# SiLU of the FFN's output moved to the FFN's end, and the gate product of the last heads moved to GpSimd

## What is computed

```python
x = L0_attn_x
xn = _layernorm(x, axis=-1)
s = _L0_attn_ref(xn, Wq, Wk, Wv, Wo, q_norm_w, k_norm_w)   # ends in out @ Wo.T
g = _silu(_L0_ffn_ref(xn, gate_w, ..., down_s))            # (silu(x@gate) * (x@up)) @ down
return x + s * g
```

## Time and profile before

| what | value |
|---|---|
| median of 3 runs | 1312.06 us (1311.99 to 1312.15) |
| the profiled execution | 1312.74 us, of which the span is 1310.9 us |
| TensorE busy | 1282.3 us, 98% of the span |
| VectorE, ScalarE, GpSimd busy | 74%, 50%, 53% |
| granted TensorE clock, mean | 0.997 |
| head, in the steady part | about 30 us |

### The profile page before, as it was taken

How to read it: one execution, slowest core, us unless ns; L and a number is a source line. 1 busy time by engine, 2 the same in 40 slices (tenths; PEclk the granted TensorE clock), 3 DMA queues, 4 the chain that set the end, 5 groups by cost and what they waited for, 6 DMA issues and landing times.

```text
span 1310.9 us, 21024 instructions
## 1 busy us (share of the span) xinstructions
PE 1282.3 (98%) x7135; PEld 1100.7 (84%) x7135; DVE 975.9 (74%) x2087; ACT 653.0 (50%) x1427; POOL 699.3 (53%) x747
## 2 busy tenths in 40 slices
PE   8999999999999999999999999999999999999996
PEld 7788888887888888888888888888888888888875
DVE  7455555577888777877787778777877787778887
ACT  4322222245565555555555555555555555555552
POOL 4755555544555455545554555455545554546444
PEclk9999999999999999999999999999999999999998
DMA  6554554020010000000000000000000000000031
GB/s 186 155 142 122 135 130 132 19 81 17 17 34 17 17 17 33 18 17 18 33 17 19 21 28 18 22 21 25 22 19 26 22 19 21 20 10 24 9 129 65
DMA packets 30909, 62.08 MB, mean 47 GB/s; under 512 B 3808, under 2 KB 3808, under 8 KB 30560
## 3 DMA queue, kind: packets, MB, share of 16 engines
q1 hardware_dynamic: 30816, 60.88, 16.1%
HBM read 56.67 MB, written 4.19 MB: 46 GB/s over the span
## 4 chain that ended last, share of the span: by engine, by line
PE 89%; DVE 6%; issue 2%; DMA 1%; POOL 1%; ACT 1%; SPq 0%; DVEq 0%; ACTq 0%; POOLq 0%
PE O L1025 31%; PE O L1086 15%; PE S L1572 11%; PE T L1046 10%; PE S L1068 5%; PE S L1066 5%; PE S L1065 5%; DVE pb L794 2%; PE T L1105 2%; PE O L1588 1%; PE T L1588 1%; PE O L1586 1%; PE T L1586 1%; PE O L1587 1%; PE T L1587 1%
## 5 line engine op out<-in xcount | busy, mean ns | idle before, releaser
L415 POOL TENSOR_TENSOR pb<-rel,coef 128x1024 f32<-128x1024 f32 (+7 forms) x256 | 293.8, 1162 | 133.0 <-PE T L1046 127.7
L536 ACT ACTIVATE pb<-pb,low 128x1024 f32<-128x1024 f32 (+7 forms) x256 | 198.9, 777 | 190.6 <-DVE low L794 188.5
L526 ACT ACTIVATE pt_h<-T 128x512 fp32r<-128x512 f32 (+3 forms) x384 | 186.0, 487 | 116.2 <-PE T L1046 113.1
L778 DVE TENSOR_TENSOR pt_l<-T,pt_h 128x512 fp32r<-128x512 f32 (+3 forms) x384 | 210.3, 550 | 40.7 <-ACT pt_h L526 40.5
L794 DVE CUSTOM_DVE_ANT_0 pb<-S,pb,ninv 128x1024 f32<-128x1024 f32 (+7 forms) x256 | 207.7, 811 | 37.8 <-PE S L1068 32.2
L1046 PE MATMUL T<-ident,pb 128*128 128x128 f32 x1152 | 189.2, 274 | 12.7 <-DVE pb L803 5.7
L1046 PEld LDWEIGHTS T<-ident,pb 128*128 128x128 f32 x1152 | 140.7, 140 | 50.8 <-issue 13.5
L803 DVE TENSOR_SCALAR pb<-pb,rinv 128x1024 f32<-128x1024 f32 (+7 forms) x256 | 171.0, 668 | 9.0
L1065 PE MATMUL S<-kT_h,q_h 128*128 128x512 f32 (+2 forms) x384 | 141.4, 368 | 0.0
L1086 PE MATMUL O<-pt_h,v_h 128*128 128x512 f32 (+2 forms) x384 | 140.6, 366 | 0.0
L375 POOL TENSOR_TENSOR wo_l<-wo_in,wo_h 128x512 fp32r<-128x512 f32 x32 | 41.6, 1298 | 181.0 <-ACT wo_h L573 181.0
(11 more groups left out here) (163 smaller groups left out, 2884.9 us busy)
## 6 DMA issues: line engine op xcount, KB each, us to landing
wq_in<-in_wq SPq DMA_DIRECT2D x32, 256.0 KB, 2.8
wo_in<-in_wo SPq DMA_DIRECT2D x32, 256.0 KB, 2.6
stage<-in_wkv SPq DMA_DIRECT2D x8, 512.0 KB, 3.9
pb<-in_gate_w SPq DMA_DIRECT2D x14, 256.0 KB, 2.6
pb<-in_gate_z SPq DMA_DIRECT2D x14, 256.0 KB, 3.6
pb<-in_gate_s SPq DMA_DIRECT2D x14, 256.0 KB, 5.0
pb<-in_up_w SPq DMA_DIRECT2D x14, 256.0 KB, 5.4
pb<-in_up_z SPq DMA_DIRECT2D x14, 256.0 KB, 6.1
```

The source lines that it names most:

```text
L415: g_.tensor_tensor(pbuf(idx, t), rel[:, TOK - w:TOK], coef[:, t:t + 1].to_broadcast([P, w]), ALU.mult).then_inc(bias_ready, 1)
L526: a_.activation(pt_lot(pt_h, t, n), bank[:, 0:m * P].rearrange("p (k w) -> p k w", w=P), ACT.Copy).then_inc(tr_hi, 1)
L536: a_.activation(pbuf(idx, t), pbuf(idx, t), ACT.Exp, bias=low[:, idx:idx + 1], scale=-1.0, accum_out=rsum[:, idx:idx + 1]).then_inc(exps_r ...
L778: v_.tensor_tensor(pt_lot(pt_l, t, n), bank[:, 0:m * P].rearrange("p (k w) -> p k w", w=P), f(pt_lot(pt_h, t, n)), ALU.subtract).then_inc( ...
```

## The change

1. SiLU is applied in place to each unit of `yT` at the FFN's end by ScalarE, right after VectorE's last sum of the unit; what goes to `y_dram` is SiLU(y). ScalarE's high part of the second group's k/v weights is made before it. There is no SiLU in the epilogue.
2. In even heads the output projections make the four units of token half 0, in odd heads those of half 1, so that the units of half 0 have their sum of heads 0 to 29 in head 30.
3. GpSimd makes x + sum x SiLU (`base`) for all eight units: unit 0 in head 30 after its last bias, units 2 and 4 in head 31 after its fourth bias, the other five after head 31's last bias. VectorE then does L994's and L997's work for all units (`finish`), and in the epilogue waits for GpSimd's base before the first of the two.
4. The loads of `x` and `y_dram` are split and partly issued in head 29. `x` goes in two halves to other places.
5. At the FFN's end TensorE's order is y units 0 to 3, scores(0, 0), y units 4 to 7, scores(0, 1), kv0, kv1, and then the transposes of tile 7. VectorE's order follows it.

```diff
+    BASES = [0, 2, 4, 1, 3, 5, 7, 6]
...
@@ SyncE @@
                 if last and j == PER - 1:
                     sp.wait_ge(out_ready, Places("last", g).n(f"qc0_{j}"))
-                    sp.wait_ge(y_out, 16 * KT * NC)
-                    sp.dma_start(keep["stage"][:, :], y_dram[:, 0:6 * CH]).then_inc(y_in, 16)
-                    sp.dma_start(xt[:, :, :], xT).then_inc(xt_in, 16)
+                    sp.dma_start(x_late[1][:, :, :], xT[:, :, CH:TOK]).then_inc(x_late_in[1], 16)
                     sp.wait_ge(tr_ready, part_no(h, "ss0") + 1)
-                    sp.dma_start(sq[:, :], y_dram[:, 6 * CH:8 * CH]).then_inc(y_in, 16)
+                    sp.dma_start(sq[:, :], y_dram[:, 6 * CH:8 * CH]).then_inc(y_in_sq, 16)
...
+                if last and j == 1:
+                    sp.wait_ge(y_out, 16 * KT * NC)
+                    sp.wait_ge(v_ready, GROUPS)
+                    sp.wait_ge(out_ready, Places("last", g).n("v1_0"))
+                    sp.dma_start(x_late[0][:, :, :], xT[:, :, 0:CH]).then_inc(x_late_in[0], 16)
+                    sp.dma_start(keep["stage"][:, :], y_dram[:, 0:6 * CH]).then_inc(y_in, 16)
...
@@ GpSimd @@
+        def base(u):
+            m, c = divmod(u, NC)
+            n = BASES.index(u)
+            pool.wait_ge(out_free, Places("last", GROUPS - 1).n(f"w{m}_{2 + c}"))
+            g_.tensor_tensor(part(sT, u), part(sT, u), y_part(u), ALU.mult).then_inc(base_ready, 1)
+            pool.wait_ge(base_ready, 2 * n + 1)
+            g_.tensor_tensor(part(sT, u), part(sT, u), x_part(u), ALU.add).then_inc(base_ready, 1)
...
                 bias(h, 2)
                 bias(h, 3)
+                if not more:
+                    base(BASES[1])
+                    base(BASES[2])
...
+                if last and j == 2:
+                    pool.wait_ge(x_late_in[0], 16)
+                    pool.wait_ge(y_in, 16)
+                    base(BASES[0])
...
         group(GROUPS - 1, "last")
-        pool.wait_ge(out_free, Places("last", GROUPS - 1).n(f"w3_{PER - 1}"))
-        pool.wait_ge(xt_in, 16)
-        for n, u in enumerate(FIN[4:]):
-            pool.wait_ge(silu_ready, 4 + n + 1)
-            g_.tensor_tensor(part(sT, u), part(sT, u), y_part(u), ALU.mult).then_inc(base_ready, 1)
-            pool.wait_ge(base_ready, 2 * n + 1)
-            g_.tensor_tensor(part(sT, u), part(sT, u), part(xt, u), ALU.add).then_inc(base_ready, 1)
+        pool.wait_ge(x_late_in[1], 16)
+        pool.wait_ge(y_in_sq, 16)
+        for u in BASES[3:]:
+            base(u)
...
@@ ScalarE @@
         steps()
+        wkv_hi_part(1)
+        silu()
...
         lots(HEADS - 1, 1)
         lots(HEADS - 1, 0)
-        silu(FIN[:4])
         v_hi(epi_at, "v0_0", PER - 1)
-        silu(FIN[4:])
...
+        def silu():
+            for u, (m, c) in enumerate(UNIT):
+                y = yT[:, m, c * CH:(c + 1) * CH]
+                act.wait_ge(y_added, (IT - 1) * UNITS + u + 1)
+                a_.activation(y, y, ACT.Silu).then_inc(silu_ready, 1)
...
@@ VectorE @@
         steps()
+        add(IT - 1, range(0, 4))
         logits(0, 0)
-        add(IT - 1, range(0, 4))
+        add(IT - 1, range(4, 8))
+        logits(0, 1)
         normalise(0, 0)
-        logits(0, 1)
-        add(IT - 1, range(4, 8))
...
-                    project(at, f"w0_{j}", unit, kind == "first")
+                    project(at, f"w0_{j}", 0 + j % 2, kind == "first")
...
+        def finish(u):
+            n = BASES.index(u)
             dve.wait_ge(out_ready, epi_at.n(f"w{u}"))
+            dve.wait_ge(base_ready, 2 * n + 1)
             v_.tensor_tensor(y_part(u), O[epi_at.bank(f"w{u}")][:, :], y_part(u), ALU.mult).then_inc(out_free, 1)
+            dve.wait_ge(base_ready, 2 * n + 2)
             dve.wait_ge(out_free, epi_at.n(f"w{u}"))
             v_.tensor_tensor(part(sT, u), part(sT, u), y_part(u), ALU.add).then_inc(fin, 1)
 
         normalise(HEADS - 1, 7)
-        project(epi_at, "w1", 1)
+        finish(1)
         lots(HEADS - 1, 1)
-        project(epi_at, "w3", 3)
+        finish(3)
         lots(HEADS - 1, 0)
-        project(epi_at, "w5", 5)
-        out_add(1)
+        finish(5)
         v_lo(epi_at, "v0_0", PER - 1)
-        out_add(3)
-        project(epi_at, "w7", 7)
-        out_add(5)
-        out_add(7)
-        for u in FIN[4:]:
-            out_last(u)
+        for u in FIN[3:]:
+            finish(u)
...
@@ TensorE @@
+        y_units(IT - 1, 1, range(0, 4))
         pe.wait_ge(sg_ready, IT * NC)
         scores(0, 0)
-        y_units(IT - 1, 1, range(0, 4))
+        y_units(IT - 1, 1, range(4, 8))
         pe.wait_ge(hid_ready, IT * NC)
         scores(0, 1)
-        y_units(IT - 1, 1, range(4, 8))
...
             if kind == "first":
-                pe.wait_ge(y_added, IT * KT * NC - 2)
+                pe.wait_ge(y_added, IT * KT * NC - 1)
+                kv_proj(at, "kv0", 1)
+                pe.wait_ge(y_added, IT * KT * NC)
+                kv_proj(at, "kv1", 1)
...
-                    project(at, f"w{n}_{j}", 4 * (j % 2) + n, h - 2 - j % 2, 0 if j >= 2 else 2,
+                    project(at, f"w{n}_{j}", 2 * n + j % 2, h - 2 - j % 2, 0 if j >= 2 else 2,
                             at.n(f"v0_{j - j % 2}"))
```

More of the change, by code:

```diff
@@ L266, in attention @@
     zeroed = sem("zeroed")
[L267 to L269 removed]
+    y_in, y_in_sq, x_late_in, base_ready, fin, stored = (
+        sem("y_in"), sem("y_in_sq"), [sem("x0_in"), sem("x1_in")], sem("base_ready"), sem("fin"), sem("stored"))
+    x_late = keep["x_late"]
     epi_at = Places("epi")
     FIN = [int(n[1]) for n in EPI if n[0] == "w"]
+    BASES = [0, 2, 4, 1, 3, 5, 7, 6]
     def part(tile, unit):
@@ L275, in part, with x_part @@
         return tile[:, m, c * CH:(c + 1) * CH]
+    def x_part(unit):
+        return x_late[unit % NC][:, unit // NC, :]
     def y_part(unit):
-        tile, n = (keep["stage"], unit) if unit < 6 else (sq, unit - 6)
+        slot = unit % NC * KT + unit // NC
+        tile, n = (keep["stage"], slot) if slot < 6 else (sq, slot - 6)
         return tile[:, n * CH:(n + 1) * CH]
@@ L620, in _ @@
         last_kv_squares()
-        weights, steps = feed.act(act)
+        weights, steps, silu = feed.act(act)
         act.wait_ge(qk_ready, 1)
@@ L649, in group @@
                     exp(h, 0)
-                elif kind != "last":
+                elif kind == "steady":
                     wkv_hi_part(g + 1)
@@ L900, in group @@
                 w = not (kind == "first" and j < 2)
-                unit = 4 * (j % 2)
                 if prev and j > 0:
@@ L937, in group @@
                 if w:
-                    project(at, f"w1_{j}", unit + 1, kind == "first")
+                    project(at, f"w1_{j}", 2 + j % 2, kind == "first")
                 if not prev:
@@ L949, in group @@
                 else:
-                    project(at, f"w2_{j}", unit + 2, kind == "first")
+                    project(at, f"w2_{j}", 4 + j % 2, kind == "first")
                 lot(h, 4, 0)
@@ L971, in group @@
                 if w:
-                    project(at, f"w3_{j}", unit + 3, kind == "first")
+                    project(at, f"w3_{j}", 6 + j % 2, kind == "first")
                 logits(h, 7)
@@ L977, in _ @@
         group(GROUPS - 1, "last")
[L978 to L985, removed]
-            v_.tensor_tensor(part(sT, u), part(sT, u), part(xt, u), ALU.add).then_inc(fin, 1)
-        def out_last(u):
-            n = FIN.index(u)
-            dve.wait_ge(silu_ready, n + 1)
-            dve.wait_ge(base_ready, 2 * (n - 4) + 1)
+        def finish(u):
+            n = BASES.index(u)
             dve.wait_ge(out_ready, epi_at.n(f"w{u}"))
+            dve.wait_ge(base_ready, 2 * n + 1)
             v_.tensor_tensor(y_part(u), O[epi_at.bank(f"w{u}")][:, :], y_part(u), ALU.mult).then_inc(out_free, 1)
-            dve.wait_ge(base_ready, 2 * (n - 4) + 2)
+            dve.wait_ge(base_ready, 2 * n + 2)
             dve.wait_ge(out_free, epi_at.n(f"w{u}"))
@@ L1264, in group @@
                 scores(h, 2)
-                if not prev:
-                    pe.wait_ge(y_added, IT * KT * NC)
-                    kv_proj(at, "kv0", 1)
                 w_unit(0)
                 lot(h, 6, 0)
-                if not prev:
-                    kv_proj(at, "kv1", 1)
                 w_unit(1)
@@ L1616, in program @@
         with ExitStack() as late:
-            late.enter_context(nc.sbuf_tensor("xt_pad", [P, KT, TOK], F32))
-            xt = late.enter_context(nc.sbuf_tensor("xt", [P, KT, TOK], F32))
+            late.enter_context(nc.sbuf_tensor("over_xh", [P, 224 + KT * TOK], F32))
+            over_xl = late.enter_context(nc.sbuf_tensor("over_xl", [P, KT, CH], F32))
+            late.enter_context(nc.sbuf_tensor("over_rest", [P, KT * CH + KT * TOK + 6 * CH], F32))
+            over_w0 = late.enter_context(nc.sbuf_tensor("over_w0", [P, KT, CH], F32))
         keep = {
-            "xt": xt,
+            "x_late": [over_w0, over_xl],
```

7 lines of the change are left out of this document (4 added, 3 removed).

## The result

The changed kernel takes 1310.28 us (median of 20 runs, 1309.46 to 1312.56), the kernel before beside it 1312.24 us (20 runs, 1311.7 to 1313.64): ratio 0.9984, 95% interval 0.9978 to 0.9991. So it is faster, by 1.96 us or 0.16%, where the prediction gave 4.6 us. That is just under the 0.2% that it had set as the bound of "faster". The profiled execution took 1310.9 us with a span of 1309.1; in the one of before the span is 1.8 us longer.

The account below looks back on a forecast made before the run. TensorE, busy 98% of the span, was taken as the bound, with time to win only where it stands still or runs slowly. Terms -7.7, +1.4, +1.6 and +0.1 took 4.6 off 1312.06: 1307.5 us, range 1304.0 to 1311.0.

Parts of the forecast that it names:

- wrong in size: Sign set beforehand: tail gain not between 5.5 and 9.5 us, or first head costing more than 2.8.
- wrong in kind: Sign set beforehand: TensorE's clock falls, or ACT's SiLUs make the first transposes late.
- rival (A): Tail: Pool still at work when the last projections come, so the tail gives 3.0 us only; 1312.1 us, chance 0.13.
- rival (B): Tail: clock falls to 1.2 GHz in idle time before head 31's values, costing 8.4 us; 1315.9 us, chance 0.08.
- The tail: Last values and projections after head 31: TensorE goes through without long waits, giving back 7.7 us, bounds 5.5 to 9.5.
- 0.3 of L803: Head 31, VectorE's multiply at 1275.75 before the transposes: it meets Pool's first operation and ends 0.3 us later.
- Pool's end: Tail: ten Pool operations behind its last bias take 16.3 us with turns given to VectorE, ending at about 1291.1.
- Heads 30 and 31: Pool's bases: 0.1 us for head 30; two multiplies held in head 31 cost 1.4 us, bounds 0.4 to 1.7.
- The end of the FFN: FFN end and first head: SiLUs hidden by 1.4 us, regrouping costs 1.6 us, bounds 0.7 to 2.8.
- The chain to the transposes of tile 5: First head: dependent steps of 6.1 us from 271.44 put these transposes at 277.55, where before they were at 275.98.
- (C): Costs before the tail are small: 0.4 us in head 31, 0.7 in the first head; 1305.6 or less, chance 0.18.
- (D): The regrouped first head costs more, 2.8 us, and head 31 its 2.0; 1309.3 us, chance 0.11.

Follow-up runs that it names:

- run 1: Changed kernel with the first head and FFN end in the order of before and no SiLU at all; 1306.48 us, ratio 0.9949 to the kernel before.
- run 5: Changed kernel with Pool's operations for units 2 and 4 made on one column only; 1308.87 us, ratio 0.9966 to the kernel before.
- run 6: Changed kernel with unit 4's base moved from head 31 to behind unit 7's, after the last bias; 1308.98 us, ratio 0.9973 to the kernel before.
- run 2: Kernel before with only the regrouped order at the FFN's end, kv0 and kv1 ahead of the first transposes, no SiLU moved; 1315.99 us, ratio 1.0026.
- run 9: Changed kernel with SiLUs kept at the FFN's end but the old order there, kv0 and kv1 between the transposes; 1312.53 us, ratio 1.0001 to the kernel before.
- run 12: The changed kernel measured again, unedited, for a second trace; 1310.13 us, ratio 0.9981 to the kernel before.
- run 3: Changed kernel with eleven unread 128x512 matmuls ahead of tile 5's transposes in head 0; 1308.62 us, ratio 0.9969 to the kernel before.
- run 4: Changed kernel with kv1 moved back between the transposes, ahead of tile 5's, kv0 staying at the front; 1307.56 us, ratio 0.9959 to the kernel before.
- run 7: Changed kernel with the bases of units 2 and 4 also behind the last bias, seven there in all; 1309.28 us, ratio 0.9975 to the kernel before.
- run 8: Changed kernel with finish cut in two, its PSUM-reading f1 ahead of the pt_l copies and f2 behind; 1308.77 us, ratio 0.9968 to the kernel before.
- run 10: Changed kernel with kv1 ahead of tile 5's transposes, unit 4's base behind unit 7's, and f1 ahead of pt_l copies; 1305.48 us, ratio 0.9948 to the kernel before.

## Why the prediction was right in sign and wrong in size

The kernel took 1310.28 us. That is inside the range of 1304.0 to 1311.0, above the 1306.0 to 1309.0 to which the forecast of 1307.5 gave 0.50, and above the 1309.4 below which it counted as faster; by that bound it was "same", which had 0.19. That the range held was partly luck: its upper end was drawn short of rival (A), which did not come. By the prediction's own signs it was wrong in size, for the first head cost 4.04 and not at most 2.8, and wrong in kind, for the clock fell, though not where rival (B) had put it.

**The tail** was worked out at -7.7 with 0.3 of L803 in it, so -8.0 from the transposes on; it measured -7.98. Its steps held too: the last values start 13.17 us after the transposes where they started 11.75 after, 1.42 later (taken: 1.75, the 2.05 less the 0.3), values and projections take 9.41 (taken: 9.0), VectorE ends 1.62 behind them (taken: 1.7), Pool's last operation ends 13.97 us after the transposes (taken: 14.5), and the clock stays 1.00. That the sum is exact is luck: 0.33 us less before the values and 0.41 more behind them cancel. Pool's end is near for a reason that was not in the working, too: the turns cost it 0.9 us where 2.6 were taken, and it stood still for 1.46 us before its seventh operation, waiting for VectorE's last `project`. Run 1 shows the term by itself. How much of it is due to the product that moved to Pool, and how much to the SiLUs that left the tail, is open: before, Pool's 17.00 us of idle time ended with ScalarE's SiLU, and no run moves one without the other.

**Heads 30 and 31**: +1.43 against +1.8 up to these transposes (1.4, 0.1 and the 0.3 of L803). The forecast said that Pool would be ahead both times, and it was. Run 5 shows the cause. The working let 0.35 of the first wait reach the second multiply; by run 6 the first costs some 0.1 us and the second 1.2. The 0.3 before the transposes came to 0.09 (0.58 us for that multiply, 0.49 before).

**The end of the FFN** is the term that failed: +1.6 was forecast, bounds 0.7 to 2.8, and it measured +4.04. Two of its steps were wrong.
- *The chain to the transposes of tile 5.* By their start the delay is 279.11 - 275.98 - 0.68 = 2.45, not 1.57 (0.68 is the first row of the books). L820 at 276.90 took 1.46 us where the working had some 0.6. The prediction knew Pool's `wq_l`, but set it at the upper bound. In the trace `wq_l` ends at 276.96 (275.68 + 1.28), 0.06 us into the multiply, and is hardly what held it. Pool's bias of 128x512 started at 276.91, 0.01 us after the multiply, and took 1.04 us (1.03 before); the multiply ended at 278.36, 0.41 us behind it, as L820 at 1269.18 ended 0.48 us behind Pool's L486. So it was the bias that went first, which the working did not have, and the bound of 2.8 held this delay by luck. The 0.6 us for the multiply was a time without Pool, and the earlier trace rows show nothing of Pool. That the meeting made the delay is read from this trace; no run took Pool's bias away.
- *The clock.* No term was there for it. After 2.89 us of idle time the next matmuls ran at 0.50, and from the transposes of tile 5 to the scores of tile 4 it took 5.04 us, not 3.42: +1.62. Runs 2, 9 and 12 show the drop again, runs 3 and 4 that it and its cost go with the gap. Not every execution has the drop: the mean granted clock was 1.000 in 4 of the 31 executions of the changed kernel (runs of 1308.64 to 1309.52 us), where the traced one, with its drop, had 0.999. The prediction had the mechanism, as rival (B), and the rows that bear on it, with an idle time "somewhere between 1.2 and 5.0 us" as the point of decision. It asked the question of the tail alone, where the forecast idle time was 1.6 us, and not of the first head, where its own working gave 2.2. That is the step that failed, a cost put at nothing without a reason: the same question was owed to every gap that the sum had made.

The SiLUs and the table load were hidden, as forecast: run 2 has the same delay of 2.45 without the move of the SiLUs. The idle 0.73 us went too.

**The rivals.** (A), Pool late, didn't come, and run 7 shows that its price was too high: 4.7 us were worked out by letting each of five held f2 delay all that follows, and three held ones cost 0.38. (Its own steps, 1294.3 + 1.7 + 4 x 2.5, end at 1306.0 and not at 1305.5.) (B) came, in another place and for 1.6 us, not 8.4: only 3 to 4 us of work ran at the half clock. The Trainium skill's rule on work moved between GpSimd and VectorE (Perfetto Trace Analysis, section Optimizing Scalar/DVE Operations) says that such a move might not help. In the tail the change as a whole did help, 24.19 us instead of 32.18 in run 1; the traces agree with the rule in the head, where Pool's two units cost 1.32 (run 5). (C) and (D) missed for the same reason as the forecast: the first head lay outside both. (D), with 0.11, named the right place and was nearest, 1309.3, but had no clock in it.

**The sum** with what was measured: -7.98 + 1.43 + 2.45 + 1.62 = -2.48 us. The medians say -1.96 and the interval is -2.9 to -1.2 us, which holds it.

## What to carry to other kernels

Price an idle time of TensorE together with the clock behind it, and ask this of every gap that a change makes, not only of the one that it is about. In this kernel a few real matmuls left between dependent steps were worth more (2.7 us) than the same matmuls done early. Where Pool and VectorE take turns, look whether the VectorE operation has slack: of two near equal waits in one head one cost 0.1 us and the other 1.2. Within a pair of operations put the one that frees PSUM, or that others wait for, ahead of the one that only finishes a sum.

## What the runs showed of the hardware

- An idle time of TensorE of 2.88 to 2.90 us before tile 5's transposes came with a granted clock of 0.50 behind it in all seven traces that have one (the changed kernel in two, runs 2, 5, 6, 7 and 8), and one of 5.09 us (run 9) too; by the mean clocks, not in every execution. After 1.64 us (runs 4 and 10), and after 1.79 us in the FFN (run 10, at 46.38), it was 1.00. In the changed kernel it was back at 1.00 by 283; work had begun again at 279.1.
- A `tensor_scalar` of 128x768 on VectorE took 1.46 us: an operation of Pool that started 0.01 us after it went first, straight behind Pool's one before. Alone such multiplies take 0.69 to 0.75 us for more elements.
- After a table load ending at 268.69 the exp started at 268.70, so the switch cost its 1.28 us and nothing behind it.
